# A two-layer graph network on one core: seven batches sum weighted input rows over the adjacency first and project the sums afterwards

## The chip, the core and the metric

The kernel runs on one core of a Trainium2 chip. Its engines each work through an instruction list of their own, in order: TensorE (PE, with its weight loads PEld) multiplies matrices into PSUM, VectorE (DVE), ScalarE (ACT) and GpSimd (POOL) work elementwise, SyncE (SP) issues nearly all transfers. Semaphores order the engines among each other. The metric is the device time of one execution in microseconds; lower is better.

## The reference, cut to what matters

Eight batches (B = 8) of N = 1024 rows with D = 128 features go through two layers, each followed by a residual and a layer norm.

```
# layer 0: masked attention
v, q, k = relu(x@Wv+bv), relu(x@Wq+bq), relu(x@Wk+bk)
att = softmax(q@k.T * adj - NEG*(1-adj))
x1 = layernorm(x + relu((att@v)@Wo + bo))
# layer 1: graph layer with additive logits
h = x1@W_w.T + W_b
e, f = h@a1, h@a2
u = adj * exp(e[:,None] + f[None,:] + a_b)
out = layernorm(x1 + (u / u.sum(axis=2)) @ h)
```

Since exp(e+f) is exp(e)·exp(f), layer 1 needs for each row n the sum over m of adj[n,m]·exp(f[m])·h[m] and the sum of the adj[n,m]·exp(f[m]) alone, its denominator.

## The kernel before

All orders are written out by hand, one list for each engine, in the functions `head` (batch 0, and what batch 1 needs of its projections), `batch_pass(p)` for p = 1 to 6, and `tail`. A pass works on the attention of batch p row block by row block (eight blocks of 128 rows), on the projections of batch p+1, and on what is left of the batches p-1 and p-2. LAST is 7.

**Attention.** `scores(p,i)` streams six 128x512 products (a high and a low part of q and k) into `s_ps`. DVE's `mask_max` adds the mask `penalty`, takes the maximum and writes `prob`; ACT's `probs` takes the exponential; `transpose_p(p,i,k)` turns four 128x128 blocks into `pt_ps[k]`; ACT's `prob_hi` and DVE's `prob_lo` split them; `attend(p,n)` runs 24 matmuls of 256 columns for two row blocks. `s_ps` and each `pt_ps[k]` exist once, so `scores(p,i+1)` waits for `mask_max(p,i)`, and `transpose_p(p,i+1,k)` for `prob_lo(p,i,k)`. ACT's `av_out` and PE's `project_out` follow, then on DVE `o_out`, `residual0` and the statistics of the first norm, POOL's `rstd0_pow`, DVE's `shift_mean0` and ACT's `norm0`, which leaves x1.

**Layer 1 of batch b.** `transpose_x1` turns x1 on PE (eight blocks), ACT's `x1t_out` takes it out, `project_h` multiplies with `w1` (128x130: the projection and the two columns of e and f), DVE's `h_out` copies, ACT's `exp_ef` takes the exponentials, `g_full` weighs each row of h with exp(f), and `g_hi`, POOL's `g_lo` and two small instructions for the denominator split that into the 258 columns of `g`. `aggregate(b,i)` (L1652) then holds a 128x128 block of the adjacency as the weights and streams the 258 columns, eight matmuls for each of the eight row blocks. DVE's `agg_out` (L1090) adds the two halves, `den_out`, `inv_den_out` and `scale_out` form the factor of each row, POOL's `residual1` (L450, L454) and `add_wb` (L445) apply it and add x1 and the bias, and statistics and `norm1` end the batch. ACT's `round_adj` makes each adjacency tile ready out of one of two staging buffers `adjt_in`; SP's `load_adj_t` fills one when it is free. The last batch does the same in pairs of row blocks, at the end of `tail`.

**Banks.** q, k, v, o, x1t, h and agg share three PSUM banks `m_ps` in the order of the `SLOTS` tables. **Queue.** SP issues in order; a load that waits for its buffer holds back all loads behind it.

## Time and profile before

| | us |
|---|---|
| median of 3 runs (395.12 to 395.23) | 395.15 |
| the profiled execution | 395.13 |
| its span, first to last instruction | 393.4 |
| PE busy | 380.5 (97%) |
| ACT busy | 329.9 (84%) |
| DVE busy | 292.8 (74%) |
| POOL busy | 279.9 (71%) |

The granted TensorE clock was 0.991 on average. Times inside the trace count from the start of the span; 1.7 us of the execution lie outside it. A matmul's own duration (290 ns for 256 columns) is longer than the distance to the next one, because matmuls overlap; what a stream costs is read from start to start.

### The profile page before, as it was taken

The page shows a single profiled execution, that of the slowest core. Times are in us where ns is not written, and L with a number is a line of the kernel's source. Part 1 is how long each engine was busy: PE and PEld are TensorE (multiplying, and loading weights), DVE is VectorE, ACT ScalarE, POOL GpSimd, SP SyncE. Part 2 cuts the span into 40 slices and gives each one's busy share as a digit, 9 for nine tenths or more (in the row PEclk, how much of TensorE's full clock was granted, in tenths as well). Part 3 has the DMA queues.
Part 4 walks back from the last instruction along what each step waited for, and adds up shares of the span by engine and source line. Part 5 has one row for each costly group of instructions (what it writes and reads, how often), then busy time and mean ns, then how long its engine had stood idle before and what let it go on. Part 6 is the DMA issues. An engine that isn't in the chain of part 4 may idle for free.

```text
span 393.4 us, 8653 instructions
## 1 busy us (share of the span) xinstructions
PE 380.5 (97%) x2757; PEld 355.2 (90%) x2757; DVE 292.8 (74%) x883; ACT 329.9 (84%) x661; POOL 279.9 (71%) x258
## 2 busy tenths in 40 slices
PE   8999999999999999999999999999999999999990
PEld 7798989989999999999999999999999999999990
DVE  3786796678668886777957887688867779697976
ACT  5877679987889887997879878898888969999962
POOL 1454951696458994789937998389956899576673
PEclk9999999999999999999999999999999999999996
DMA  8945533807657168754597266780676647978011
GB/s 259 376 166 166 164 129 137 328 38 268 200 185 314 61 235 260 262 203 171 175 292 298 84 240 215 243 322 13 253 214 233 252 162 285 386 224 282 4 55 53
DMA packets 38156, 80.71 MB, mean 205 GB/s; under 512 B 2785, under 2 KB 19681, under 8 KB 38113
## 3 DMA queue, kind: packets, MB, share of 16 engines
q1 hardware_dynamic: 37824, 80.03, 58.3%
q8 instruction: 23, 0.38, 0.4%
q10 hardware_dynamic: 288, 0.14, 0.1%
q14 instruction: 21, 0.16, 0.1%
HBM read 75.96 MB, written 4.19 MB: 204 GB/s over the span
## 4 chain that ended last, share of the span: by engine, by line
PE 91%; DVE 5%; issue 2%; POOL 0%; ACT 0%; POOLq 0%; DVEq 0%; ACTq 0%
PE pt_ps L1612 14%; PE m_ps L1660 13%; PE s_ps L1541 8%; PE av_ps L1625 8%; PE av_ps L1626 8%; PE av_ps L1624 8%; PE s_ps L1543 7%; PE s_ps L1542 7%; PE m_ps L1583 4%; PE m_ps L1649 3%; PE m_ps L1633 3%; PE m_ps L1541 2%; PE m_ps L1542 2%; PE m_ps L1543 2%; PE m_ps L1640 2%
## 5 line engine op out<-in xcount | busy, mean ns | idle before, releaser
L1033 DVE TENSOR_TENSOR prob_tl<-pt_ps,prob_th 128x512 fp32r<-128x512 f32 x128 | 85.5, 684 | 29.8 <-ACT prob_th L670 29.6
L1025 DVE CUSTOM_DVE_ANT_0 prob<-s_ps,penalty 128x1024 f32<-128x1024 f32 x64 | 78.0, 1218 | 30.8 <-PE s_ps L1543 26.2
L670 ACT ACTIVATE prob_th<-pt_ps 128x512 fp32r<-128x512 f32 x128 | 74.7, 596 | 21.0 <-PE pt_ps L1612 20.8
L405 POOL TENSOR_SCALAR penalty<-raw 128x1024 bf16<-128x1024 f32 x64 | 66.4, 1047 | 28.3 <-DMA raw<-in_adj_dram 13.2
L662 ACT ACTIVATE prob<-prob,neg_max 128x1024 f32<-128x1024 f32 x64 | 73.8, 1153 | 1.4 <-DVE neg_max L1025 1.3
L1624 PE MATMUL av_ps<-prob_th,vh 128*128 128x256 f32 x256 | 74.1, 290 | 0.0
L1612 PE MATMUL pt_ps<-rhs,prob 128*128 128x128 f32 x512 | 73.2, 273 | 0.0
L1626 PE MATMUL av_ps<-prob_th,vl 128*128 128x256 f32 x256 | 72.4, 283 | 0.0
L1625 PE MATMUL av_ps<-prob_tl,vh 128*128 128x256 f32 x256 | 72.4, 283 | 0.0
L607 ACT ACTIVATE adj_t<-adjt_in 128x1024 fp32r<-128x1024 f32 x56 | 59.3, 1061 | 11.2 <-PE m_ps L1660 11.1
L1612 PEld LDWEIGHTS pt_ps<-rhs,prob 128*128 128x128 f32 x512 | 60.1, 141 | 4.1
L1660 PE MATMUL m_ps<-g,adj_t 128*128 128x258 f32 x448 | 63.2, 288 | 0.0
L1660 PEld LDWEIGHTS m_ps<-g,adj_t 128*128 128x128 f32 x448 | 57.9, 190 | 1.5
L1541 PE MATMUL s_ps<-kh,qh 128*128 128x512 f32 x128 | 53.5, 418 | 0.7 <-DVE neg_max L1025 0.6
L1543 PE MATMUL s_ps<-kh,ql 128*128 128x512 f32 x128 | 50.3, 393 | 0.0
L1542 PE MATMUL s_ps<-kl,qh 128*128 128x512 f32 x128 | 50.1, 392 | 0.0
L1625 PEld LDWEIGHTS av_ps<-prob_tl,vh 128*128 128x128 f32 x256 | 49.0, 191 | 0.0
L1624 PEld LDWEIGHTS av_ps<-prob_th,vh 128*128 128x128 f32 x256 | 49.0, 191 | 0.0
L1626 PEld LDWEIGHTS av_ps<-prob_th,vl 128*128 128x128 f32 x256 | 48.9, 191 | 0.0
L450 POOL TENSOR_TENSOR gs<-gs,scale 128x512 f32<-128x512 f32 x14 | 14.6, 1040 | 35.4 <-DVE scale L1103 35.4
L1090 DVE TENSOR_REDUCE gs<-m_ps 128x129 f32<-128x258 f32 x59 | 24.4, 416 | 7.2 <-PE m_ps L1660 7.1
L1541 PEld LDWEIGHTS s_ps<-kh,qh 128*128 128x128 f32 x128 | 24.1, 188 | 5.7 <-DVE neg_max L1025 0.9
(139 smaller groups left out, 785.2 us busy)
## 6 DMA issues: line engine op xcount, KB each, us to landing
raw<-in_adj_dram SPq DMA_DIRECT2D x64, 512.0 KB, 5.6
adjt_in<-in_adj_t_dram SPq DMA_DIRECT2D x56, 512.0 KB, 3.9
x_in<-in_x_dram SPq DMA_DIRECT2D x8, 512.0 KB, 6.2
raw<-in_adj_t_dram SPq DMA_DIRECT2D x8, 512.0 KB, 5.7
out_dram<-out_sb SPq DMA_DIRECT2D x14, 256.0 KB, 4.5
xt_odd<-in_x_t_dram SPq DMA_DIRECT2D x8, 256.0 KB, 5.2
raw<-in_x_t_dram SPq DMA_DIRECT2D x7, 256.0 KB, 4.7
out_dram<-out_sb SPq DMA_DIRECT2D x4, 128.0 KB, 1.8
```

Source lines behind the costliest of these rows:

```text
L662: sc.activation(prob[i % 2][:, :], prob[i % 2][:, :], ACT.Exp, bias=neg_max[:, i:i + 1], scale=-1.0, accum_out=row_sum[b % 2][:, i:i + 1]) ...
L670: sc.activation(prob_th[n % 2][:, tiles(k), (i % 2) * P:(i % 2 + 1) * P], pt_ps[k][:, :].rearrange("p (c n) -> p c n", n=P), ACT.Copy).the ...
L1025: v.tensor_tensor_reduce(out=prob[i % 2][:, :], in0=s_ps[:, :, :].rearrange("p a n -> p (a n)"), in1=penalty[:, n % RING, :], scale=-1.0, ...
L1033: v.tensor_tensor(prob_tl[n % 2][at], pt_ps[k][:, :].rearrange("p (c n) -> p c n", n=P), prob_th[n % 2][at].bitcast(F32), ALU.subtract).th ...
L1541: pe.matmul(dst, lh, rh, start=True, stop=False)
L1542: pe.matmul(dst, lh, rl, start=False, stop=False)
L1543: return pe.matmul(dst, ll, rh, start=False, stop=True)
L1612: last = pe.transpose(blk(pt_ps[k], c), blk(prob[i % 2], k * TH + c), ident)
L1624: pe.matmul(av_ps[:, 0:PAIR], vh[:, c, :], th[:, c, :], start=(c == 0), stop=False)
L1625: pe.matmul(av_ps[:, 0:PAIR], vh[:, c, :], tl[:, c, :], start=False, stop=False)
L1626: last = pe.matmul(av_ps[:, 0:PAIR], vl[:, c, :], th[:, c, :], start=False, stop=(c == T - 1))
L1660: last = pe.matmul(a[:, 0:2 * G1], adj_tile(b, i)[:, c, :], g[:, c, :, :].rearrange("p a e -> p (a e)"), start=(c == 0), stop=(c == T - 1))
```

## The change

For the batches 0 to 6 the order of layer 1 is turned round. The adjacency sums the weighted rows exp(f)·x1 themselves; the sums, 128 features by 1024 rows, come out already transposed, and the projection is applied to them. `transpose_x1`, `x1t_out`, `project_h`, `h_out`, `g_hi_den`, `g_lo_den` and POOL's `residual1` and `add_wb` go for these batches.

- e and f are row products on DVE (`weigh`): sixteen multiply-and-add reductions a batch of a 128x128 tile of x1 with one of two constant tiles (`a_rows`), the result of each one column of `dots`.
- `g_full` writes 127 weighted feature columns and, in place of the last one, the weight exp(f) itself; the constant `w_sum` (128x129, from `raw_wd`) undoes this and carries the bias and the denominator. `form_sets` on PE, `place_rows` and `place_sets` on DVE make these constants once, in `head`.
- `aggregate` holds a 128x128 part of g (high or low) as the weights and streams 512 columns of the adjacency: four matmuls for each of eight tiles, two sums of 512 rows. The adjacency comes in another layout, in transfers of the same size. ACT's `sums_out` takes a sum out, `project_sum` multiplies it with `w_sum`.
- `den_out`, `inv_den_out` and `scale_out` now come for each pair of row blocks, 128x2, four of each a batch; `residual1` is a DVE instruction for each row block that reads PSUM. x1 has two buffers.
- All order lists and bank tables are written anew. The last batch keeps its method.

```diff
+            def weigh(b, k):
+                dve.wait_ge(x1_done, T * b + (k + 1) * TH)
...
+                for t in range(k * TH, (k + 1) * TH):
+                    for r in range(2):
+                        v.tensor_tensor_reduce(out=blk(x1t, 2 * (t % TH) + r), in0=x1_in[b % 2][:, t, :], in1=a_rows[r], scale=1.0,
+                                               scalar=0.0, op0=ALU.mult, op1=ALU.add,
+                                               accum_out=dots[:, t, r:r + 1]).then_inc(dots_done, 1)
...
+            def residual1(b, j):
...
+                for c in range(2):
+                    t = 2 * j + c
+                    last = v.scalar_tensor_tensor(out=gs[:, t, 0:D], in0=bank["p", b, j][:, c * G1:c * G1 + D],
+                                                  scalar=scale1[:, t:t + 1], in1=x1_in[b % 2][:, t, :],
+                                                  op0=ALU.mult, op1=ALU.add)
...
-                for c in range(T):
-                    last = pe.matmul(a[:, 0:2 * G1], adj_tile(b, i)[:, c, :],
-                                     g[:, c, :, :].rearrange("p a e -> p (a e)"), start=(c == 0), stop=(c == T - 1))
+                    for r in range(2):
+                        last = pe.matmul(a[:, :], g[:, 2 * c2 + c, r, 0:D], half(adj_tile(b, i), c),
+                                         start=(i % TH == 0 and c == 0 and r == 0), stop=(i % TH == TH - 1 and c == 1 and r == 1))
...
+            def project_sum(b, j):
+                pe.wait_ge(ut_done, 2 * b + j // 2 + 1)
+                out_rows = shared("p", b, j)
+                for c in range(2):
+                    last = pe.matmul(out_rows[:, c * G1:(c + 1) * G1], blk(ut, 2 * j + c), w_sum, start=True, stop=True)
...
+            def sums_out(b, h):
+                act.wait_ge(agg_full, T * b + TH * (h + 1))
+                sc.activation(half(ut, h), bank["agg", b, h][:, :], ACT.Copy).then_inc(ut_done, 1)
```

Of SP's list in a pass, two lines of it:

```diff
+                load_adj_t(p - 1, 0)
+                if there(p - 2):
+                    load_adj_t(p - 2, 7)
...
-                if there(p - 2):
-                    load_adj_t(p - 2, 7)
-                load_adj_t(p - 1, 0)
```

**PE in a pass**, from the projection of q of the next batch on (its rows read `m_ps<-xth,w_hl`), first before, then now; `s_ps` rows are `scores`, `pt_ps` rows `transpose_p`, and two full-precision rows are one `project_*` call.

```order
L1543 MATMUL m_ps<-xth,w_hl 128x512
L1660 MATMUL m_ps<-g,adj_t 128x258 x16
L1612 MATMUL pt_ps<-rhs,prob 128x128 x4
L1583 MATMUL m_ps<-wb,raw 128x128 x2
L1660 MATMUL m_ps<-g,adj_t 128x258 x8
L1612 MATMUL pt_ps<-rhs,prob 128x128 x4
L1541 MATMUL s_ps<-kh,qh 128x512
```

```order
L1567 MATMUL m_ps<-xth,w_hl 128x512
L1668 MATMUL m_ps<-adj_t,g 128x512 x8
L1565 MATMUL s_ps<-kh,qh 128x512
...
L1668 MATMUL m_ps<-adj_t,g 128x512 x4
L1636 MATMUL pt_ps<-rhs,prob 128x128 x4
L1678 MATMUL m_ps<-sets,ut 128x129 x2
```

Eight narrow matmuls a row block became four wide ones a tile, and the projection of the sums follows where there was none.

**DVE in a pass**, from `mask_max(p,5)` (the `ISA prob,neg_max` row) to behind `mask_max(p,6)`, first before, then now; `x1t,dots` rows are `weigh`, here four row blocks of it, each product followed by a read of the accumulator.

```order
L1025 ISA prob,neg_max<-s_ps,penalty 128x1024
L1025 ISA neg_max 128x1
L1033 TENSOR_TENSOR prob_tl<-pt_ps,prob_th 128x4x128
L1080 COPY h_sb<-m_ps 128x260
L1108 BN_STATS stat<-gs 128x6 x4
L1025 ISA prob,neg_max<-s_ps,penalty 128x1024
```

```order
L1004 ISA prob,neg_max<-s_ps,penalty 128x1024
L1004 ISA neg_max 128x1
L1012 TENSOR_TENSOR prob_tl<-pt_ps,prob_th 128x4x128
L1102 BN_STATS stat<-gs 128x6 x4
L1064 ISA x1t,dots<-x_in,sets 128x128
L1064 ISA dots 128x1
...
L1004 ISA prob,neg_max<-s_ps,penalty 128x1024
```

Between two `mask_max` one copy went and eight products with eight reads came; another eight stand between `mask_max(p,4)` and `mask_max(p,5)`.

**SP at the start**, first before, then now; `raw<-in_x_t_dram 128x256` are the two quarters of x that the first projections wait for, `raw<-in_adj_dram` is a 512 KB tile of the mask, `wb` holds weights.

```order
L275 DMA raw<-in_x_t_dram 128x256 x2
L281 DMA raw<-in_x_t_dram 128x512
L284 DMA wb<-in_pack_b_dram 128x640
L255 DMA raw<-in_adj_dram 128x1024 x2
L288 DMA x_in<-in_x_dram 128x8x128
L281 DMA xt_odd<-in_x_t_dram 128x512 x2
```

```order
L258 DMA raw<-in_adj_dram 128x1024
L278 DMA raw<-in_x_t_dram 128x256 x2
L284 DMA raw<-in_x_t_dram 128x512
L258 DMA raw<-in_adj_dram 128x1024
L287 DMA wb<-in_pack_b_dram 128x640
L258 DMA raw<-in_adj_dram 128x1024
```

A mask tile moved ahead of the quarters, and the weights moved behind a second tile, whose buffer has to be free first (POOL's first `convert` frees it).

## Rows read from the trace of the kernel before

**Rows 1.** Busy time by stretch (us; instructions in brackets), granted clock, DMA share.

```profile
131.50:177.83 46.33, 46.33 (x342) 43.58 (x341) 35.09 (x104) 39.98 (x80) 37.13 (x34) 1.00 0.62 217
...
345.00:366.00 21.00, 20.97 (x166) 20.20 (x166) 16.96 (x61) 20.97 (x37) 13.25 (x11) 1.00 0.71 231
366.00:380.00 14.00, 13.17 (x108) 12.40 (x106) 11.49 (x52) 12.55 (x41) 11.44 (x12) 1.00 0.01 2
```

**Rows 2.** PE in order of time: start, duration, line, tiles.

```profile
228.57 0.28 PE L1624 MATMUL av_ps<-prob_th,vh 128*128 128x256 f32 x1
...
231.45 0.40 PE L1541 MATMUL s_ps<-kh,qh 128*128 128x512 f32 x1
...
232.83 1.12 PE L1660 MATMUL m_ps<-g,adj_t 128*128 128x258 f32 x8
233.79 0.60 PE L1612 MATMUL pt_ps<-rhs,prob 128*128 128x128 f32 x4
234.22 0.61 PE L1633 MATMUL m_ps<-wb,av 128*128 128x128 f32 x4
234.67 0.60 PE L1612 MATMUL pt_ps<-rhs,prob 128*128 128x128 f32 x4
```

**Rows 3.** All engines at the start, in order of time (idle time before, releaser).

```profile
0.79 0.85 SPq L275 DMA_DIRECT2D raw<-in_x_t_dram  x2
...
3.51 0.95 ACT L616 ACTIVATE xth<-raw 128x256 fp32r<-128x256 f32 x2 [0.52 <-DMA raw<-in_x_t_dram]
...
4.76 0.55 PE L1541 MATMUL m_ps<-xth,w_hl 128*128 128x256 f32 x1
...
12.79 1.23 DVE L1025 CUSTOM_DVE_ANT_0 prob<-s_ps,penalty 128x1024 f32<-128x1024 f32 x1 [0.87 <-issue]
...
14.08 0.50 PE L1541 MATMUL s_ps<-kh,qh 128*128 128x512 f32 x1
...
15.91 1.23 DVE L1025 CUSTOM_DVE_ANT_0 prob<-s_ps,penalty 128x1024 f32<-128x1024 f32 x1 [0.88 <-PE s_ps L1543]
```

**Rows 4.** Busy time and, last, GB/s of the fourth microsecond.

```profile
3.00:4.00 1.00, 1.00 (x7) 1.00 (x6) 0.24 (x2) 0.42 (x1) 0.00 (x0) 1.00 1.07 372
```

**Rows 5.** DVE in order of time, in one pass.

```profile
226.31 1.12 DVE L1047 SCALAR_TENSOR_TENSOR m_ps<-m_ps,inv_sum,wb 128x128 f32<-128x128 f32 x4
227.34 1.21 DVE L1025 CUSTOM_DVE_ANT_0 prob<-s_ps,penalty 128x1024 f32<-128x1024 f32 x1
228.48 0.08 DVE L1025 DVE_READ_ACCUMULATOR2_ANT neg_max<- 128x1 f32 x1
228.48 0.42 DVE L1054 SCALAR_TENSOR_TENSOR x<-m_ps,x_in 128x256 f32<-128x256 f32 x1
228.93 0.87 DVE L1060 BATCH_NORM_STATS2 stat<-x 128x6 f32<-128x128 f32 x4
229.72 1.32 DVE L1033 TENSOR_TENSOR prob_tl<-pt_ps,prob_th 128x512 fp32r<-128x512 f32 x2
230.96 0.15 DVE L1039 RECIPROCAL inv_sum<-row_sum 128x2 f32<-128x2 f32 x1
231.03 0.40 DVE L1054 SCALAR_TENSOR_TENSOR x<-m_ps,x_in 128x256 f32<-128x256 f32 x1
```

**Rows 6.** DVE groups by line and shape: busy us, mean ns of one, idle before.

```profile
L1025 DVE CUSTOM_DVE_ANT_0 prob<-s_ps,penalty 128x1024 f32<-128x1024 f32 x64 | 78.0, 1218 | 30.8 <-PE s_ps L1543 26.2 <-PE pt_ps L1612 2.3 <-issue 2.0
...
L1090 DVE TENSOR_REDUCE gs<-m_ps 128x129 f32<-128x258 f32 x59 | 24.4, 416 | 7.2 <-PE m_ps L1660 7.1
...
L1047 DVE SCALAR_TENSOR_TENSOR m_ps<-m_ps,inv_sum,wb 128x128 f32<-128x128 f32 x64 | 18.8, 348 | 0.5 <-PE m_ps L1633 0.5
...
L1183 DVE SCALAR_TENSOR_TENSOR gs<-gs,scale,x1b 128x128 f32<-128x128 f32 x8 | 2.3, 346 | 0.0
```

**Rows 7.** The chain that ended last, in the tail: start, us, what.

```profile
365.79 0.60 DVE prob_tl L1033
...
374.85 0.41 PE m_ps L1669 x2
```

More of the change, by code:

```diff
@@ L811, in head @@
                 av_out(0, 1)
+                v_relu(1, 2)
+                k_out(1, 1)
                 prob_hi(0, 5, 0)
@@ L1325, in batch_pass @@
-                if there(p - 2):
-                    agg_out(p - 2, 4)
+                if there(p - 2):
+                    scale_out(p - 2, 0)
+                prob_lo(p, 2, 0)
+                inverse_sum(p, 0)
+                if there(p - 2):
+                    residual1(p - 2, 0)
+                v_bias(p + 1, 0)
+                mask_max(p, 4)
                 shift_mean0(p - 1)
                 if there(p - 2):
-                    agg_out(p - 2, 5)
-                inverse_sum(p, 0)
@@ L1340, in batch_pass @@
                 prob_lo(p, 3, 0)
                 if there(p - 2):
-                    inv_den_out(p - 2)
+                    residual1(p - 2, 1)
+                weigh(p - 1, 0)
+                inverse_sum(p, 1)
                 if there(p - 2):
-                    scale_out(p - 2)
+                    inv_den_out(p - 2, 2)
                 prob_lo(p, 3, 1)
+                if there(p - 2):
+                    scale_out(p - 2, 2)
+                if there(p - 2):
+                    residual1(p - 2, 2)
@@ L1408, in tail @@
+                residual1(LAST - 2, 0)
                 prob_lo(LAST, 2, 0)
[L1409 to L1411 removed]
+                prob_lo(LAST, 2, 1)
+                weigh(LAST - 1, 0)
                 mask_max(LAST, 4)
[L1413 to L1416 removed]
+                weigh(LAST - 1, 1)
                 prob_lo(LAST, 3, 0)
+                den_out(LAST - 2, 2)
@@ L1432, in tail @@
-                prob_lo(LAST, 5, 0)
+                mask_max(LAST, 7)
+                prob_lo(LAST, 5, 1)
+                inverse_sum_pair(2)
+                prob_lo(LAST, 6, 0)
+                stats0_pair(0)
                 mean_var1(LAST - 2, 1)
-                stats0_pair(0)
+                prob_lo(LAST, 6, 1)
+                o_out(LAST, 1)
+                residual0(LAST, 1)
                 var_eps1(LAST - 2)
-                prob_lo(LAST, 5, 1)
-                mask_max(LAST, 7)
@@ L1731, in form_w1, with form_sets @@
                 pe.matmul(av_ps[:, E1:2 * E1], wb_wide[:, :], rhs1[:, :], start=True, stop=True).then_inc(set_full, 1)
+            def form_sets():
+                pe.wait_ge(wd_ok, 4)
+                pe.wait_ge(wc_ok, 3)
+                out_rows = shared("set", 0, 1)
+                for r in range(2):
+                    pe.matmul(blk(out_rows, r), a_wide[:, r, :], raw_wc[:, :], start=True, stop=True).then_inc(set2_full, 1)
+                pe.matmul(blk(out_rows, 2), raw_wd[:, :], ident, start=True, stop=True).then_inc(set2_full, 1)
             def head():
```

1002 lines of the change are left out of this document (494 added, 508 removed), and 9 rows, old and new, of tables (HEAD_SLOTS, PASS_SLOTS).

## The prediction

> **What bounds the kernel now.** I read the busy time by stretch first [rows 1]. In one pass, 46.33 us long, PE is busy for all 46.33; ACT has 39.98, POOL 37.13, DVE 35.09, and the granted clock is 1.00. PE is thus the bound of the six passes, and what is taken from its list shortens them as long as no other engine becomes late. In the tail this changes: from 345 to 366 ACT is busy for 20.97 of 21.00 us, as full as PE, and from 365.8 to 374.8 the chain of waits begins with a DVE instruction and reaches PE only at 374.85 [rows 7]. A saving on PE there is worth nothing by itself. At the start the first projection of PE is at 4.76, behind ACT's copy of a quarter of x (3.51), which waited for its transfer [rows 3].
>
> **What PE loses and gets.** The costs go from start to start [rows 2]. Four transposes take 0.43 to 0.44, from 233.79 to 234.22; an aggregate of one row block (eight matmuls, 258 columns) takes 233.79 − 232.83 = 0.96; six products of 512 columns take 232.83 − 231.45 = 1.38, so 0.23 each; a full-precision call of two 128-wide blocks takes 234.67 − 234.22 = 0.45.
> - The transposes of x1: seven batches of two go, 14 × 0.44 = −6.2.
> - The sums: 56 × 0.96 = 53.9 becomes 224 matmuls × 0.229 = 51.3, so −2.6 to −2.8.
> - The projection: 28 calls of 0.45 become 28 calls of the same kind with 129 columns, 0.
> - The constants: three full-precision products in the head, half of 0.45 each, +0.7.
>
> The sum is **−8.3**. By place: pass 1 loses transposes and projections of batch 0, whose new projection comes later, −0.9 − 1.8 = −2.7; passes 2 to 6 lose 0.9 + 0.4 each, −6.4; the tail exchanges about the same; the head +0.7. A pass then has 45.0 of PE.
>
> **The head: +0.8.** A 512 KB mask tile now goes before the quarters of x. At 372 GB/s [rows 4] it takes 1.4 us, so the first projection can move from 4.76 to about 6.2. Also, the weights wait behind a second tile that needs a freed buffer. For this, ACT, DVE and PE get a new order in the head whose gain the trace doesn't show; PE is nowhere idle long after the first `mask_max` (12.79 to 15.91 is a loop of 1.83 for scores and start of `mask_max`, and 1.29 back [rows 3]). Bounds: 0, if the new order takes all of it back, and +2.5, if the 1.4 stay and the weights cost another microsecond. I take 0.8, nearer to a part regained.
>
> **The six passes: +1.2.** Other engines must keep up with a pass of 45.0.
> - ACT exchanges two copies of 128x512 (`x1t_out`) for two of the same size (`sums_out`): about 40 of 45, nothing to pay.
> - POOL loses two kinds of instruction and gets none: it is looser than before.
> - DVE loses eight `agg_out` of 0.416 [rows 6] and four copies of about the same width, −5.0. It gets eight `residual1` at 0.26 (four `o_out`, which read PSUM too, take 227.34 − 226.31 = 1.03), +2.1; some nine small instructions at 0.07 (230.96 to 231.03), +0.6; and sixteen `weigh`. All rows of this: [rows 5].
>
> What one `weigh` costs, call it w, no row shows: a multiply with a sum, 128 columns, both operands in SBUF, then a read of the accumulator. From below: a statistics instruction of 128 columns takes 0.79 / 4 = 0.20. `mask_max` (1024 columns, also with an accumulator read) takes 1.14 and `prob_lo` (512) 0.62, so 1.0 ns a column, and 1.14 − 896 × 0.00102 = 0.23 for 128 columns. In that place the read has a duration of 0.08, but the next instruction starts in the same instant, 228.48. From above: 0.26 as `o_out`, plus 0.08 if the read isn't overlapped, 0.34. I take 0.23, since `mask_max` is the nearest kind. So DVE has 35.1 − 5.0 + 2.1 + 0.6 + 16 × 0.23 = 36.5 of 45: on average loose.
>
> But the products stand in two lumps of eight, between `mask_max(p,4)` and `(p,5)` and between `(p,5)` and `(p,6)`, and scores and transposes have one buffer each. So I count one stretch: from the start of `scores(p,4)` to the end of the `prob_lo` that `transpose_p(p,5,1)` needs. DVE: 1.83 to the first `mask_max`, three of them 3.42, five `prob_lo` 3.1, eight small 0.56, a 256-wide step 0.42, four `residual1` 1.04, statistics 0.79, together 11.2 + 16 w. PE in the same stretch: three scores 4.14, five calls of 0.45, five groups of transposes 2.2, two `attend` of 231.45 − 228.57 = 2.88 [rows 2], one projection 0.69, together 15.0. With w = 0.23 DVE has 14.9: just in time. From w = 0.24 on each pass waits 16 (w − 0.24). As so little is left I add 0.2 us for small waits in each pass, 1.2 in all. Bounds: 0, and at w = 0.34, 6 × 1.6 = 9.6.
>
> A rule speaks against the new products here. Two instructions with the same 128 columns, one with an operand in PSUM (L1047) and one with both fp32 operands in SBUF (L1183), take 348 and 346 ns [rows 6]: the place of the operands changes nothing. The Trainium skill, "Vector Engine (DVE) Microarchitecture Reference", section 7 on points easy to get wrong, says that a two-input instruction of the scalar-tensor kind with two SBUF operands that are not bf16 runs at half throughput. These rows disagree with it.
>
> **The tail: +1.8.** ACT, full there, gets four `sums_out` (batches 5 and 6) for two `x1t_out`; two more of 512 columns at about 0.62 (DVE's 512-wide `prob_lo` [rows 5]), less a few small steps: +0.8 in 345 to 366. In the DVE stretch from 365.8 on, the `agg_out` of batch 6 leave, but eight `residual1` (2.1) and twelve small ones (0.8) come, behind a copy and a projection; I count a third of the 2.9, +1.0, on the chain. Bounds: 0 (all beside PE's last sums), and +2.9 + 0.8 = 3.7.
>
> **Forecast.** The profiled execution took 395.1 (span 393.4 and 1.7 around it), which is the median of the runs. 395.1 − 8.3 + 0.8 + 1.2 + 1.8 = **390.6**.
>
> **Rivals.**
> 1. *Everything is covered.* Head, waits and tail cost nothing: 395.1 − 8.3 = 386.8. For it: 8 us a pass spare on DVE and 5 on ACT. Against: ACT's full stretch in the tail, and the mask tile ahead of the quarters.
> 2. *Order and transfers eat the gain.* In five passes the load of the last adjacency tile of a batch now stands behind the first tile of the next. If `aggregate(p-2,7)` finds its tile late by up to a tile's 1.4 us, 0 to 7.0 is lost; from 0.9 a pass on hardly anything is left of the gain. Taken at 0.95: 390.6 + 4.7 = 395.3, no change. Against: PE reads a batch's eight tiles over a whole pass, so a tile is loaded long before its use; the DMA share in a pass is 0.62 [rows 1].
> 3. *The lump of `weigh` stops the score loop: slower.* The forecast's gain of 4.5 is used up at 96 (w − 0.24) = 4.5, w = 0.287. At w = 0.32 (`o_out` and most of the read) it is 390.6 + 7.7 = 398.3, and at 0.34 400.2. For it: the read of the accumulator comes here after each 128 columns, not after 1024, and nobody has seen it so close together. Against: 228.48, where it costs nothing.
> 4. *The products take two passes over their operands*, 128 × 1.0 ns = 0.13 more, w = 0.36: 390.6 + 96 × 0.12 = 402.1. Against: 346 and 348 ns. It is what the halving in that section of the Trainium skill would do here; no row bears it out.
>
> **Chances.** Forecast (388 to 393.5) 0.47; rival 1 0.20; rival 2 0.13; rival 3 0.17; rival 4 0.03. About 0.2% (0.8 us) is what a measurement of this kernel can tell from no change. Rival 2 lies on both sides of that band: about half in it, half still faster. So faster 0.73, same 0.07, slower 0.20. The range: below, rival 1 with a little more, 386.5; above, 398.5, which takes in w up to 0.32 and leaves out the rest of rivals 3 and 4, about 0.1 at either end.
>
> **What would show it.** In the profile after: a pass of 45.0 to 45.3 with PE busy in nearly all of it; sums at 0.23 a matmul; `weigh` at 0.23 from start to start. PE's first projection near 6 instead of 4.76. If w is 0.26 or more, PE waits in each pass for `neg_max` or for `prob_lo` around the blocks 5 and 6, and only there. If rival 2 holds, the last sum of a batch waits for ACT's `round_adj`, and that for a transfer. If the tail is mis-sized, the stretch from the last `prob_lo` of attention to the end, 393.4 − 365.8 = 27.6 now, has grown by something other than 1 us. I would be wrong most of all if the new order shortens a stretch that is not bound by PE, the head or the DVE stretch of the tail: I count no gain there.

## The result and the profile after

The changed kernel takes **407.72 us** (median of 4 runs, 404.39 to 409.53) against 395.19 of the kernel before: ratio 1.031, 95% interval 1.024 to 1.038. It is slower by 3.1%; I had said 390.6, in a range of 386.5 to 398.5. The profiled execution, the slowest of the four, took 409.53 (span 407.8; before 393.4). Its page, busy time, granted clock in 40 slices and the chain that ended last, by engine:

```profile
PE 381.2 (93%) x2483; PEld 336.9 (83%) x2483; DVE 320.8 (79%) x1141; ACT 332.0 (81%) x668; POOL 232.6 (57%) x223
...
PEclk9989999999999999999999999999999999999996
...
PE 47%; DVE 17%; DMA 11%; ACT 10%; issue 7%; POOL 1%; SPq 1%; DVEq 0%; POOLq 0%; ACTq 0%
```

The chain is the first thing to see. PE is still the fullest engine, but the chain runs through PE in 47% of the span only; before it was 91%. PE has gone from bound to one of several that wait for each other. The waits of PE, the largest and one more (line, what it waited for: us in total, times, longest):

```profile
PE m_ps L1668 <- ACT adj_t L589: 3.4, 3, 1.4
PE m_ps L1755 <- ACT raw L635: 3.2, 1, 3.2
PE m_ps L1565 <- DVE w_hl L1204: 2.4, 1, 2.4
...
PE m_ps L1678 <- ACT ut L669: 1.2, 2, 0.8
```

And by stretch, as [rows 1]: busy time, granted clock, DMA share.

```profile
0.00:10.00 10.00, 6.18 (x26) 5.37 (x27) 2.75 (x10) 4.23 (x7) 1.79 (x8) 0.92 0.69 229
10.00:20.00 10.00, 8.75 (x49) 7.04 (x47) 8.67 (x13) 6.67 (x13) 6.16 (x5) 0.90 0.76 272
20.00:30.00 10.00, 7.79 (x34) 6.44 (x35) 7.41 (x16) 5.33 (x11) 3.27 (x4) 0.83 0.52 174
...
256.70:303.70 47.00, 45.88 (x303) 40.69 (x302) 37.88 (x141) 40.27 (x80) 30.39 (x29) 1.00 0.59 208
```

In the first 30 us PE is idle for more than 7 and the granted clock is below 1.00; a pass of 47.00 has PE busy for 45.88.

A ruler for everything below: when PE starts the first `attend` of batch 0, 1 and 7, when it starts the last `attend`, and the span. Each is given against the kernel before (22.9, 61.5, 337.9, 367.3 and 393.4), from the profiled execution of each version. Batch 1 closes the head, batch 7 the six passes. It is one execution of each, and the same lists don't give the same times twice: with the head of the changed kernel left as it is, batch 0 stands at +10.3 (the changed kernel), +8.5, +9.8, +8.1 and +8.5 (`e4_swap`, `e5_port`, `e6_bench`, `e7_tail`). In this head a difference of under 2 us between single executions says little.

```
version      batch 0  batch 1  batch 7  last attend  span
after         +10.3     +8.4    +10.5      +9.9     +14.4
e1_loads       +6.7     +4.7     +7.1      +6.8     +11.0
e2_sets        +6.7     +5.4     +8.4      +7.9     +12.2
e3_head        +0.3     +3.5     +4.6      +3.8      +8.2
e4_swap        +8.5     +6.5     +5.4      +4.5      +8.5
e5_port        +9.8     +7.8     +5.0      +3.9      +7.9
e7_tail        +8.5     +6.5     +5.1      +5.1      +9.0
e8_head        +2.3     +2.1     +3.2      +2.3      +6.5
e9_stt         -0.4     +0.2     -0.9      -2.3      +1.8
e11_tail       +0.2     +0.8     -0.3      -1.7      +1.7
e12_all        +0.1     +0.6     -0.4      -0.2      +3.8
e14_act        +0.5     +1.0     -1.9      -2.3      +2.2
e13_order      -0.3     +0.3     -2.6      -3.2      +1.7
e15_all        +0.1     +0.7     -2.3      -2.7      +0.1
e16_all        -0.2     +0.3     -2.8      -2.7      -1.4
```

So of the 14.4 in this execution 8.4 come from the head, 2.1 from the six passes (where I expected −7.9), −0.7 from the last batch's attention, and 4.6 from what follows the last `attend`.

**The head**, all engines in order of time:

```profile
5.79 0.72 ACT L598 ACTIVATE xth<-raw 128x256 fp32r<-128x256 f32 x2 [2.80 <-DMA raw<-in_x_t_dram]
...
6.83 0.29 DVE L1204 TENSOR_TENSOR w_hl<-wa,w_hl 128x128 fp32r<-128x128 f32 x1
...
7.18 0.39 PE L1565 MATMUL m_ps<-xth,w_hl 128*128 128x256 f32 x1 [2.41 <-DVE w_hl L1204]
```

```profile
16.33 1.69 DVE L992 TENSOR_TENSOR ql<-raw,qh 128x512 fp32r<-128x512 f32 x1
17.95 2.29 DVE L1227 COPY a_wide<-wa 128x128 f32<-128x128 f32 x2
20.16 1.09 DVE L1228 TENSOR_SCALAR raw_wd<-wb 128x127 f32<-128x127 f32 x1
...
22.20 1.19 PE L1755 MATMUL m_ps<-raw_wc,a_wide 128*128 128x128 f32 x4 [3.23 <-ACT raw L635]
...
24.05 0.63 PE L1566 MATMUL s_ps<-kl,qh 128*128 128x512 f32 x1
24.47 0.63 PE L1567 MATMUL s_ps<-kh,ql 128*128 128x512 f32 x1
```

The first projection starts at 7.18 instead of 4.76 [rows 3], since ACT's quarter of x lands behind the mask tile and the split of the weights stands behind it on DVE. Then DVE makes the constants, slowly (two copies of 128 columns in 2.29; one at 7.92 took 0.22), and PE stands 3.23 us before `form_sets`. Behind that wait products of 512 columns come every 0.42 (24.05 to 24.47) where the same ones take 0.23 [rows 2]. The granted clock there (the third figure from the end) is 0.50, the lower of the two levels 1.2 and 2.4 GHz:

```profile
22.20:25.50 3.30, 3.29 (x11) 2.91 (x12) 2.10 (x5) 2.24 (x5) 1.05 (x1) 0.50 0.88 291
```

This doesn't follow every such wait. `e4_swap` has the same head and waits 2.26 at the same place, up to 21.88; behind it the clock is full:

```profile
21.90:26.00 4.10, 4.10 (x24) 3.29 (x25) 3.60 (x9) 2.81 (x6) 1.11 (x2) 1.00 1.00 356
```

**A pass**, SP, ACT and PE in order of time:

```profile
149.02 0.81 SPq L263 DMA_DIRECT2D adjt_in<-in_adj_t_dram  x2
```

```profile
154.87 1.06 ACT L589 ACTIVATE adj_t<-adjt_in 128x1024 fp32r<-128x1024 f32 x1 [1.64 <-DMA adjt_in<-in_adj_t_dram]
```

```profile
155.98 1.20 PE L1668 MATMUL m_ps<-adj_t,g 128*128 128x512 f32 x4 [1.05 <-ACT adj_t L589]
```

SP issues two adjacency tiles together, the first of the next batch ahead of the last of this one. ACT and then PE wait for the second one. The same stands at 250.12 (1.38) and 297.14 (0.93): this is my second rival, as I had described it.

### The profile page after: what moved, and what is told of

Read it like the earlier page. It is cut to its first block, busy times and chain, and to the rows that moved or that the text cites. A ratio compares the mean times of both kernels' runs of the same rounds, so it can differ in the third digit from the quotient of the medians.

```text
span 407.8 us, 8276 instructions
## 1 busy us (share of the span) xinstructions
PE 381.2 (93%) x2483; PEld 336.9 (83%) x2483; DVE 320.8 (79%) x1141; ACT 332.0 (81%) x668; POOL 232.6 (57%) x223
## 4 chain that ended last, share of the span: by engine, by line
PE 47%; DVE 17%; DMA 11%; ACT 10%; issue 7%; POOL 1%; SPq 1%; DVEq 0%; POOLq 0%; ACTq 0%
DMA adjt_in<-in_adj_t_dram 10%; PE pt_ps L1636 8%; PE m_ps L1668 6%; PE s_ps L1565 5%; PE s_ps L1566 4%; PE s_ps L1567 4%; ACT adj_t L589 4%; PE av_ps L1649 4%; PE av_ps L1648 4%; PE av_ps L1650 4%; DVE x1t L1064 3%; DVE prob L1004 3%; DVE prob_tl L1012 2%; PE m_ps L1657 2%; DMA raw<-in_adj_t_dram 2%
## 5 line engine op out<-in xcount | busy, mean ns | idle before, releaser
L1004 DVE CUSTOM_DVE_ANT_0 prob<-s_ps,penalty 128x1024 f32<-128x1024 f32 x64 | 78.1, 1220 | 35.9 <-PE s_ps L1567 29.9
L408 POOL TENSOR_SCALAR penalty<-raw 128x1024 bf16<-128x1024 f32 x64 | 67.4, 1059 | 36.5 <-DMA raw<-in_adj_dram 21.9
L1636 PE MATMUL pt_ps<-rhs,prob 128*128 128x128 f32 x512 | 75.0, 274 | 1.1 <-DVE prob_tl L1012 0.6
L1668 PE MATMUL m_ps<-adj_t,g 128*128 128x512 f32 x224 | 61.0, 408 | 3.4 <-ACT adj_t L589 3.4
L1565 PE MATMUL s_ps<-kh,qh 128*128 128x512 f32 x128 | 54.8, 428 | 1.3 <-DVE neg_max L1004 0.9
L427 POOL CAST kh<-raw 128x512 fp32r<-128x512 f32 x14 | 8.2, 615 | 78.1 <-PE s_ps L1567 78.1
L1668 PEld LDWEIGHTS m_ps<-adj_t,g 128*128 128x128 f32 x224 | 39.8, 189 | 12.6 <-ACT adj_t L589 5.2
L435 POOL TENSOR_TENSOR vl<-raw,vh 128x512 fp32r<-128x512 f32 x16 | 20.7, 1295 | 15.0 <-ACT vh L640 15.0
```

Source lines behind the costliest of these rows:

```text
L408: gp.tensor_scalar(penalty[:, n % RING, :], adj_in[:, n % RING, :], PENALTY, -PENALTY, ALU.mult, ALU.add).then_inc(penalty_done, 1)
L1004: v.tensor_tensor_reduce(out=prob[i % 2][:, :], in0=s_ps[:, :, :].rearrange("p a n -> p (a n)"), in1=penalty[:, n % RING, :], scale=-1.0, ...
L1565: pe.matmul(dst, lh, rh, start=True, stop=False)
L1636: last = pe.transpose(blk(pt_ps[k], c), blk(prob[i % 2], k * TH + c), ident)
L1668: last = pe.matmul(a[:, :], g[:, 2 * c2 + c, r, 0:D], half(adj_tile(b, i), c), start=(i % TH == 0 and c == 0 and r == 0), stop=(i % TH == ...
```

## The experiments

Beside each the kernel before ran on the same chip (395.0 to 395.2).

**The head: three undos.** `e1_loads` gives SP's list at the start its old order:

```diff
 def head():   # SP
-    load_adj(0, 0)
-    load_x_t_quarter(1)
     load_x_t_quarter(0)
+    load_x_t_quarter(1)
     load_x_t(0, 1)
...
```

> The changed kernel, with only SP's load order of the head put back to the order of before (quarters of x first, weights early). Theory (the head lost 10.3 us, by three separate causes: late quarters and weights, constants in DVE's way, and the half clock that follows each wait of PE): the first projection moves from 7.18 back to about 5, the slow stretch of matmuls from 8.6 to 11.6 goes, the wait of 3.2 us for form_sets stays; the first attend moves from 33.2 to 29.5 or 30, time about 404. Rival (the loads are covered by the later waits of the head): the first projection moves, the first attend stays within 1 us of 33.2, time 407 to 408.

405.79, ratio 1.027 (1.024 to 1.030). `e2_sets` only moves `place_rows`, `form_sets` and `place_sets` to the end of the head:

> The changed kernel, with the making of the constants (place_rows and place_sets on DVE, form_sets on PE) moved from the start of the head to its end. Theory (DVE's three copies of the constants, slowed beside POOL to about 1 us each, hold back v_bias, the second mask_max and so PE for 3.2 us, and the half clock that follows costs another 1.5): first attend from 33.2 to about 28.5, time about 403. Rival (it is the slow stretch of DVE beside POOL, whatever stands there): less than 2 us of it come back, 406 or more.

405.08, 1.024 (1.021 to 1.026). In these executions batch 1 comes 3.7 and 3.0 earlier; in the medians the kernels gain 1.9 and 2.6, and their intervals overlap with that of the changed kernel. Both times missed the theory (404 and 403) and lie between it and the rival. `e1_loads` still waits 2.85 before `form_sets`, but with the full clock behind it, so a part of its gain may be the clock's. Neither run alone settles a cause; what follows does. `e3_head` has the whole head of before, with the constants late:

> The changed kernel with the whole head in the order of before on all five engines, the constants behind it (place_rows late in the head, form_sets at its end, place_sets in pass 1). Theory (the head's order alone is worth 9 to 10 us): the first attend is at 23 to 24, and the gain is kept: time 398 to 399, still over 395, since passes gain nothing and the tail loses. Rival (the lists of pass 1 need the new head, or the passes take it back by waits of their own): over 402.

403.70, 1.022 (1.020 to 1.023): batch 0 as forecast (+0.3), batch 1 at +3.5, so the time missed the expected 398 to 399 by 5 us and is the rival's. The constants had found the next bad place, in front of a `mask_max` that PE waits for. DVE:

```profile
35.58 1.33 DVE L1227 COPY a_wide<-wa 128x128 f32<-128x128 f32 x1
36.83 1.09 DVE L1228 TENSOR_SCALAR raw_wd<-wb 128x127 f32<-128x127 f32 x1
```

Here too each of them takes over 1 us. `e8_head` (with the swap of `e4_swap`, below) lets ACT make the constants:

```diff
 def head():   # ACT
     q_out(0, 1)
+    place_rows()      # as activations
 def head():   # PE
     transpose_p(0, 0, 1)
+    form_sets()
```

> The load order of e4_swap, the whole head in the order of before, and the constants made on ACT (five small instructions behind the second q_out), the three products behind the first transposes. Theory (the head loses by order, and by DVE making constants beside POOL): no wait of PE over 0.5 us in the head, the first attend at 23.5 to 24, that of batch 1 at 62.5 to 63 where e3_head had 65.0; time 398.5. Rival (the lists from pass 1 on need the other head): batch 1 at 64 or later, 400 or more.

399.12, 1.010 (1.008 to 1.012), near the 398.5 of the theory and 6.4 us better than `e4_swap`. A wait of 1.56 was left right behind `form_sets`; with that put to the end of the head (in `e9_stt`) batch 1 is at +0.2. The 8.4 us of the head were the order, and which engine makes the constants; the half clock went with them.

**The passes: two loads.** `e4_swap`, two lines of SP's list:

```diff
+    if there(p - 2):
+        load_adj_t(p - 2, 7)
     load_adj_t(p - 1, 0)
-    if there(p - 2):
-        load_adj_t(p - 2, 7)
```

> The changed kernel with two lines of SP's list of a pass in the order of before: the load of the last adjacency tile of a batch ahead of the first one of the next batch. Theory (the load of tile 7 waits behind one that needs a later round_adj, and shares the queue with it: 1.05, 1.38 and 0.93 us of waiting on PE in three passes): these three waits go, time 404 to 405. Rival (another wait ends a little later in the same place, PE's list is held by DVE or ACT): the waits for adj_t go, the period of the passes stays, 407.

405.48, 1.027 (1.022 to 1.033). The medians are 2.2 apart and the intervals overlap; in the profiled executions, all passes at a granted clock of 1.00, the six passes go from +2.1 to −1.1 in the table. The three waits are gone, but a pass is 46.65 (three from 167.82 to 307.76), longer than before. What is left are two waits in each pass, 0.38 for `prob_tl` and 0.36 for `neg_max`. Just ahead of them, DVE and POOL:

```profile
209.18 0.28 DVE L1064 CUSTOM_DVE_ANT_0 x1t<-x_in,sets 128x128 f32<-128x128 f32 x1
...
209.38 1.12 DVE L1064 CUSTOM_DVE_ANT_0 x1t<-x_in,sets 128x128 f32<-128x128 f32 x1
...
210.43 0.28 DVE L1064 CUSTOM_DVE_ANT_0 x1t<-x_in,sets 128x128 f32<-128x128 f32 x1
```

```profile
209.20 1.15 POOL L464 TENSOR_TENSOR out_sb<-out_sb,rstd 128x512 f32<-128x512 f32 x1
```

Fifteen products start 0.21 apart, one takes 1.05, and it ends when POOL's normalisation ends. `e5_port` moves that POOL instruction from there:

```diff
     norm1(p - 3, 0)
+    norm1(p - 3, 1)
     v_lo(p, 1)
...
     q_lo(p + 1, 0)
-    norm1(p - 3, 1)
     k_hi(p + 1, 0)
```

> The load order of e4_swap, and on POOL the second half of norm1 of a pass moved directly behind its first half, away from the time in which DVE runs the first eight products of weigh. In e4_swap one product of each pass took 1.12 us in place of 0.28 and ended with POOL's norm1 instruction, and PE then waited for prob_lo and neg_max, 1.17 us a pass beyond its work. Theory (a DVE instruction with both operands in SBUF waits for POOL's running instruction, and that makes the stall): no product of weigh near 209 is long, the two waits shrink from 1.17 to under 0.4 a pass, about 4 us less than e4_swap, time 400 to 401. Rival (DVE is simply too full there, w is over 0.24): the long product goes, and the waits of PE stay over 0.8 a pass, 404 or more.

403.59, 1.024 (1.018 to 1.031, widened by one run of 408.96); a pass 46.20 instead of 46.65, the long product gone, one wait of 0.2 a pass left. The mechanism is as the theory has it; the 400 to 401 was missed: the six passes gained 1.6 (−1.1 to −2.8 in the table), not 4.

**What POOL holds on DVE.** `e6_bench` puts rows of DVE instructions behind the kernel's end, alone and beside POOL (482.3 with them).

> The changed kernel with extra DVE and POOL work on scratch tiles behind its end: seven forms of DVE instruction (weigh, a copy, statistics, scalar-tensor with one PSUM operand, the same with two SBUF operands, a 512-wide subtraction with one PSUM operand and one with two SBUF operands), first alone, then beside a row of 24 POOL subtractions of 512 columns, then beside 24 POOL converts. Its total says nothing on the change. Theory (DVE and POOL exclude each other where DVE reads two SBUF operands or copies in SBUF, not where one operand is in PSUM): weigh 0.21 alone and about 1.2 beside POOL, the copy and the two-operand forms likewise, the forms with a PSUM operand and the statistics as fast as alone. Rival (a general contention): all forms get slower by a like factor, none waits for a whole POOL instruction.

DVE alone, then beside POOL's 512-wide subtractions, then (last row) beside its `convert`; what one instruction of a row costs is read from start to start:

```profile
403.69 0.28 DVE L1264 CUSTOM_DVE_ANT_0 x1t<-x_in,sets 128x128 f32<-128x128 f32 x1
...
403.90 1.17 DVE L1267 COPY ut<-x_in 128x128 f32<-128x128 f32 x8
...
416.95 1.33 DVE L1264 CUSTOM_DVE_ANT_0 x1t<-x_in,sets 128x128 f32<-128x128 f32 x1 [1.37 <-POOL xtl L490]
...
418.22 1.34 DVE L1264 CUSTOM_DVE_ANT_0 x1t<-x_in,sets 128x128 f32<-128x128 f32 x1
...
427.09 9.81 DVE L1267 COPY ut<-x_in 128x128 f32<-128x128 f32 x8
436.82 1.63 DVE L1269 BATCH_NORM_STATS2 stat<-x_in 128x6 f32<-128x128 f32 x8
438.37 2.14 DVE L1271 SCALAR_TENSOR_TENSOR gf<-m_ps,minus_half,x_in 128x128 f32<-128x128 f32 x8
440.43 2.18 DVE L1274 SCALAR_TENSOR_TENSOR xt_odd<-x_in,minus_half 128x128 f32<-128x128 f32 x8
...
470.76 4.74 DVE L1274 SCALAR_TENSOR_TENSOR xt_odd<-x_in,minus_half 128x128 f32<-128x128 f32 x8
```

A copy of 128 columns goes from 0.14 to 1.22, a product of `weigh` from 0.21 to 1.27: each stands for a whole POOL instruction (1.24). Statistics (0.20) and the form that reads PSUM (0.26) don't change. The Trainium skill, "SBUF — State Buffer", section "SBUF: two separate sides", says that the two engines share a pair of ports under a lock that lasts a whole instruction, taken by VectorE in a two-port mode or with two SBUF inputs, and that whichever starts first has it. The copy and the product agree with it. So does the last form (two SBUF inputs), with the roles changed: beside the subtractions it keeps its 0.27, and it is POOL that waits, two subtractions in 4.51 instead of 2.48:

```profile
438.00 2.48 POOL L490 TENSOR_TENSOR ql<-prob 128x512 fp32r<-128x512 f32 x2
440.45 4.51 POOL L490 TENSOR_TENSOR kl<-prob 128x512 fp32r<-128x512 f32 x2
```

Beside `convert` it takes 0.59. Why the copy loses in such a row and this form wins, no run shows; and it doesn't always win, as `e15_all` shows below. The kernel before had the effect too, in its tail. A shift of two columns, also a scalar-tensor instruction with two SBUF operands, took 0.93 beside POOL, where the next one takes 0.13 (375.55):

```profile
368.66 1.19 POOL L454 TENSOR_TENSOR gs<-gs,x1b 128x512 f32<-128x512 f32 x1
368.94 0.93 DVE L1143 SCALAR_TENSOR_TENSOR shift<-mv,rstd 128x2 f32<-128x2 f32 x1
```

Is it the product's special instruction? `e9_stt` (`e8_head`, `form_sets` late, and the products as the ordinary form):

```diff
-v.tensor_tensor_reduce(out=..., in0=x1_in[...], in1=a_rows[r], scale=1.0, scalar=0.0,
-                       op0=ALU.mult, op1=ALU.add, accum_out=dots[:, t, r:r + 1])
+v.scalar_tensor_tensor(out=..., in0=x1_in[...], scalar=1.0, in1=a_rows[r],
+                       op0=ALU.mult, op1=ALU.mult, accum_out=dots[:, t, r:r + 1])
```

> As e8_head (load order of e4_swap, head of before, constants made on ACT; here the three products that form the constants stand late in the head, before the second q projection of batch 1), and weigh written as a scalar-tensor-tensor instruction with a sum in place of the custom multiply-and-reduce. The bench showed the custom form to wait for a whole POOL instruction each time (1.27 us in place of 0.21) and the scalar-tensor form with the same two SBUF operands not to (0.26 beside POOL subtractions). Theory (the stall of the passes is this exclusion, not the number of products): with 0.26 a product, dearer than 0.21 alone, the long product of 1.1 us goes, and so do most of the waits of 1.17 us a pass for prob_lo and neg_max; the passes go from 46.65 to 46.0 or less, time 396 to 397. Rival (DVE is too full, a product of 0.26 makes it worse): the waits stay or grow, the passes stay at 46.6 or more, 399 or more.

398.04, 1.007 (1.005 to 1.010). The product still starts 0.21 after the other, and one in a pass still takes 1.12 (156.61, 203.22, 249.86, 296.47); PE's waits are what they were. My theory on the form fell: with a constant as scalar and a sum as second result the ordinary form waits for POOL too. What the profile shows as gained is 1.9 in the head, and a wait of 1.40 at 331.14 in `e8_head`, for an adjacency tile that landed late.

**The tail.** After the last `attend` come 30.6 us instead of 26.0. `e7_tail` (on `e4_swap`) gives the last batch its own `ef` tile and puts the products of its first two pairs into the two score banks, the first pair ahead of the last `attend`:

```diff
-            ("h_last", LAST, 0), ("x1t", LAST, 2), ("h_last", LAST, 1), ("o", LAST, 3), ...
+            ("x1t", LAST, 2), ("o", LAST, 3), ...
+        bank["h_last", LAST, 0], bank["h_last", LAST, 1] = s_ps[:, 0, :], s_ps[:, 1, :]
```

> The load order of e4_swap, and in the tail the exponentials of the last batch in a tile of their own (so that they need not wait for the factors of the batch before), and the products of its first two pairs in the two score banks, the first ahead of the last attend (so that they need not wait for residual1 of the batch before). Theory (the tail's 3.9 us are the last batch's chain held up by the sums of batch 6 through one tile and three shared banks): the stretch from the last attend to the end goes from 30.0 in e4_swap to 27 or 28, time 403. Rival (DVE's added work of batch 6 is the bound there, whatever the banks): under 0.8 us, 405.

405.69, 1.026 (1.023 to 1.029); 29.9 us remain, as the rival has it. But a new wait of 2.15 for `residual0` stands at 382.62 in this execution, with the clock at 0.50 behind it, so the run alone doesn't show that tile and banks cost nothing. `e11_tail` (`e9_stt` with the first form of `weigh`) takes POOL's normalisation of batch 6, beside which DVE's short instructions took about 1 us, to ACT:

```diff
-    norm1(LAST - 1, 0)      # POOL
-    norm1(LAST - 1, 1)
+    norm1_rows(0)           # ACT, behind g_hi_pair(3)
...
+    norm1_rows(1)
```

> As e9_stt but with the custom weigh again, and norm1 of batch 6 moved from POOL to ACT (eight scalings with a bias, as the last batch has them), so that POOL runs no 512-wide instruction beside DVE's small ones at the end. Theory (the tail lost 3.9 us mostly because POOL's norm1 of batch 6, which came later with the projection of the sums, now runs beside the last chain and holds DVE's small SBUF instructions, five of 0.7 to 1.0 us in place of 0.15): those five are short, the stretch from the last attend to the end goes from 30.0 to 27 or 27.5, time 396. Rival (DVE's own added work is the bound): they are short, but the stretch stays over 29, 398 or more.

396.82, 1.005 (1.004 to 1.007); 29.5 us remain, again as the rival has it, though the time is nearer to the theory's. `e12_all` joins all of this:

> All parts that helped together, on the method of the change: the load order of e4_swap, the head of before with the constants made on ACT, POOL's norm1 away from weigh as in e5_port, and a tail in which norm1 of batch 6 is on ACT, the last batch's exponentials have their own tile and the score banks, and DVE does the last residual0 ahead of the statistics of batch 6. Theory (the method saves some 8 us of PE's work, and what ate it are order, exclusion of DVE and POOL, and waits): passes at 46.1 or less, the stretch from the last attend to the end 27.5 or less, time 391.5 to 393, under before. Rival (DVE's added work is the bound of the passes and of the tail, so the method is worth nothing here): 395 or more.

397.71, 1.006 (1.004 to 1.008). Missed by 5: batch 6's attention starts 1.4 earlier than in `e11_tail`, and the tail lost it in four waits of 0.83 to 1.31. Its trace named them: ACT's copies `round_adj` and `round_last` stood waiting for their transfers in front of steps that PE needed, and DVE had batch 6's statistics in front of the last batch's `g`. `e14_act` moves only those ACT copies (three places like this one):

```diff
-    round_adj(LAST - 2, 6)
     sums_out(LAST - 2, 0)
     probs(LAST, 1)
+    round_adj(LAST - 2, 6)
```

> The version with all repairs (shown above: 397.71, profiled 398.92, span 397.2), with ScalarE's list alone changed at three places of the tail: a copy that rounds an adjacency tile and stood waiting for its transfer (1.83 us at 325.66, 1.07 at 334.81, 0.69 at 364.08) goes behind the steps that others wait for (sums_out, probs, prob_hi). Theory (late engines in front of TensorE, not TensorE's own work, make the tail longer): TensorE's waits of 1.21 at 327.3, 0.41 at 337.2 and 0.83 at 366.3 go; the start of the last attend moves from 367.1 to about 365; from there to the end 30.1 as now, since VectorE's list is untouched: 395.5 to 396.5. Rival (the last batch's own chain sets the end, and what ends before it counts for nothing): the last attend moves, the end does not: 397.5.

397.19, 1.005 (1.004 to 1.007). The last `attend` came 2.1 earlier than in `e12_all`, the span shrank by 1.6, the median by 0.5: between the theory (395.5 to 396.5) and the rival (397.5), nearer to the rival. `e13_order` also takes batch 6's statistics off that stretch of DVE and gives the last batch its own result tiles:

```diff
-    stats1(LAST - 1, 0)      # DVE, behind residual1(LAST - 1, 1)
...
     var_eps0_pair(3)
+    stats1(LAST - 1, 0)
     g_lo_den_pair(2)
     g_lo_pair(2)
+    stats1(LAST - 1, 1)
```

> As the run with ScalarE's list changed, and also: VectorE's statistics of batch 6 (16 bn_stats and bn_aggr and what follows, 2.4 us) move out of the stretch between the last attention and the last batch's g into the gaps behind it (2.4 us of them from 377 to 381), for which the last batch gets its own result tiles. Theory (in that stretch VectorE is the bound, because batch 6's residual and denominators came into it: 2.1 + 0.6 us more than before): TensorE's waits of 1.31 at 377.1 and 1.29 at 382.3 go, from the last attend to the end 27.5 to 28 instead of 30.1, 26.1 before the change; time 392.5 to 394, below the 395.0 of the kernel before. Rival (TensorE's and ScalarE's own work there sets the length): 29.5 or more from the last attend to the end, 395 to 396.

396.91, 1.005 (1.004 to 1.007). Both DVE waits went and the last batch's first sum came at 373.45 (375.48 in `e14_act`, 377.14 in `e12_all`), but the end stayed, because a third wait took their place. PE, then a stretch with its clock:

```profile
375.52 0.71 PE L1714 MATMUL m_ps<-w,x1t 128*128 128x130 f32 x4 [1.34 <-ACT x1t L707]
375.99 0.91 PE L1746 MATMUL s_ps<-g,adjt_last 128*128 128x258 f32 x4
376.69 1.06 PE L1746 MATMUL pt_ps<-g,adjt_last 128*128 128x258 f32 x4
377.55 1.06 PE L1746 MATMUL s_ps<-g,adjt_last 128*128 128x258 f32 x4
```

```profile
375.50:379.00 3.50, 3.48 (x19) 3.48 (x20) 2.68 (x14) 3.47 (x14) 0.86 (x1) 0.62 0.01 2
```

Behind a wait of 1.34 four products take 0.86 instead of 0.48, at a granted clock of 0.62. `e15_all` takes this wait away (ACT's `norm0_pair(1)` and `round_last(6)` later), gives the last results a tile of their own and puts POOL's power for batch 6 ahead of its additions:

```diff
     x1t_out_pair(2)
-    norm0_pair(1)
     exp_ef_pair(2)
...
     g_hi_pair(3)
+    norm0_pair(1)
```

> As the run with VectorE's statistics moved (396.9, span 395.1: VectorE's waits in front of TensorE were gone there and the first product of the last batch came at 373.45 instead of 377.14, but a copy of x1 on ScalarE, held 1.71 us by norm0_pair(1), kept TensorE waiting 1.34 at 375.52, behind which the products ran at 0.215 instead of 0.12 until 379; at 389.86 ScalarE waited 3.27 for a store of batch 6). Three repairs: norm0_pair(1) and the copy of adjacency tile 6 go behind the steps that TensorE waits for; POOL makes batch 6's deviation ahead of its additions; the last batch's results go to a tile of their own. Theory (late engines, one behind the other, and the half clock that follows a wait, are all that separates this version from the saving): TensorE's waits of 0.87 at 369.3 and 1.34 at 375.5 go, with the slow stretch 3.5 us in all, of which part is lost to the chain at the end: 392.0 to 393.5, first version below the kernel before (395.0). Rival (the last chain on VectorE from the first sum to the end, 14.4 us in e13_order and 12.8 before, stays bound to its own instructions): 395 to 396.

395.28, 1.000 (0.999 to 1.001): even with the kernel before, not below it, as the rival has it. In the last chain two DVE instructions stood beside POOL's additions:

```profile
380.35 1.25 DVE L1217 SCALAR_TENSOR_TENSOR shift<-mv,rstd 128x8 f32<-128x8 f32 x1 [0.16 <-POOL rstd L464]
...
381.79 1.45 DVE L1197 SCALAR_TENSOR_TENSOR gs_l<-gs_l,scale,x_in 128x128 f32<-128x128 f32 x2
```

```profile
380.28 2.54 POOL L454 TENSOR_TENSOR x_in<-x_in,wb_row 128x512 f32<-128x512 f32 x2
```

Without POOL beside them the shift takes 0.16 (`e13_order`, 383.15) and two such residuals 0.59 (383.96). The residual is the form that kept its 0.27 in `e6_bench`, with a scalar from a tile and two SBUF operands.

`e16_all`:

```diff
-    rstd1_pow(LAST - 1)      # POOL
     add_wb(0)
+    rstd1_pow(LAST - 1)
...
-    round_last(6)            # ACT
     exp_ef_pair(3)
...
-    shift6()                 # DVE, ahead of scale_pair(0)
     stats1_pair(0)
+    shift6()
```

> As e15_all (395.3; no wait of TensorE but 1.00 at 377.85 is left in the tail, and TensorE ends its work at 382.6, 1.1 earlier than before the change, but the end is the same). In VectorE's last chain two instructions stood beside POOL's addition of 380.2 to 381.5: the shift of batch 6 took 1.25 instead of 0.16 and a residual 1.45 instead of 0.60. Changed: the copy of adjacency tile 6 behind the last exponentials (TensorE's wait of 1.00), the shift of batch 6 behind the first statistics of the last chain, POOL's first addition ahead of its power. Theory (VectorE held by POOL, and one late copy, are what is left): 1.0 + 1.1 + 0.9 less what comes new: 392.5 to 393.5, below the kernel before (395.0). Rival (the end is set by the length of the last chain itself, about 12.5 us from its first sum): the first sum can come at most 1.0 earlier: 394.3.

**393.72** (393.46 to 393.94), ratio 0.9966 (0.9954 to 0.9978): between theory and rival, nearer to the theory, and the first version that beats both kernels, the one before by 0.3%. Its page and the largest waits of PE behind the preparation of 1.4 us, which the kernel before has too:

```profile
PE 376.6 (96%) x2483; PEld 334.6 (85%) x2483; DVE 316.5 (81%) x1138; ACT 334.8 (85%) x681; POOL 227.0 (58%) x219
...
PE 66%; DVE 20%; issue 6%; ACT 3%; DMA 2%; SPq 1%; POOL 1%; DVEq 0%; POOLq 0%; ACTq 0%
```

```profile
PE s_ps L1581 <- DVE neg_max L1027: 1.1, 4, 0.4
PE s_ps L1581 <- DVE ql L1015: 0.9, 1, 0.9
PE s_ps L1744 <- DVE g L1171: 0.4, 1, 0.4
```

Even here the chain runs through PE in 66% only. And the 1.4 us are not the method's alone: several of the repairs (batch 6's norm on ACT, the last batch's own tiles, the later copies) don't depend on it, and no run gives them to the kernel before.

## Why the prediction was wrong

By place, in the profiled execution: the passes +2.1 where I had −7.9, the head +8.4 where I had +1.5 (0.8 and the constants' 0.7), the tail +3.9 where I had +1.8. So the six passes are the step that failed most (by 10.0), then the head (6.9), then the tail (2.1). In all three I priced the waits too low, and in the passes the saving too high.

**PE's saving, −8.3: too large.** `e16_all` hardly waits, so its steady pass (46.16, from 199.66 to 245.82) can be set against one of before (46.32, 200.94 to 247.26), start to start, idle time taken out:

```
in one pass                  before        e16_all
transposes of x1              0.87            -
sums                          8.04           7.68
projection (16 products)      1.63           1.87
everything else              35.78          36.39
idle                          0.00           0.22
```

Transposes and sums are as I counted them (−0.87 and −0.36 against −0.87 and −0.4; 56 × 0.96 is 53.8, not 53.9, which is little). The projection, which I set at 0, costs +0.24; so the pass has −1.0 of work where I wrote −1.3. Then the same products of attention and projections take 0.60 more from start to start, 0.41 of it in the scores and 0.19 in `attend`, and 0.22 is idle: −0.16 a pass is left. Over all six passes `e16_all` is 3.1 shorter than before, 1.2 of it in the first and 1.2 in the last.

**The passes, +1.2 of waits: 2.1 lost where −7.9 was forecast.** Of the 10.0 the two lines of SP's list are 3.3 (`e4_swap`) and POOL's instruction beside `weigh` 1.6 (`e5_port`); the other 5.1 are mostly saving that even `e16_all` doesn't show (−3.1 against −7.9). Two causes of waits, one of them on my list.
- Rival 2 (0.13) was right in mechanism and place: three waits of 0.93 to 1.38. My reason against it, that "a tile is loaded long before its use", is refuted by 154.87: the tile was used as soon as it landed. ACT frees a staging buffer at 148.99, and only then, at 149.02, SP can issue.
- Rival 3's place was right and its mechanism wrong. w is 0.21 from start to start (I took 0.23), the read of the accumulator costs nothing, and no second pass over the operands shows, so rivals 3 and 4 fall as written (`e6_bench`: eight scalar-tensor instructions with one operand in PSUM 2.14, with both in SBUF 2.18). But one product of sixteen stood 1.05 beside POOL. That is 0.84 in a stretch that I had at 14.9 against 15.0, "just in time"; in `e4_swap` PE's waits there came to 0.74 a pass. The trace of before had a sign of it that I overlooked (0.93 at 368.94, beside POOL), and I counted POOL only as "looser than before".

**The head, +0.8: 8.4.** I saw the mask tile ahead of the quarters and priced it at 1.4 of transfer; the first projection came 2.4 later. I named 0 and +2.5 as bounds from the transfer alone and let "the new order" of the other engines take some back. The order was the cost: the wait of 3.23 before `form_sets`, DVE's constants beside POOL, and, in this execution, half clock behind the two long waits. `e8_head` and `e9_stt` show it by undoing it (+2.1 and +0.2).

**The tail, +1.8: 3.9 (−0.7 and +4.6).** The added work on DVE was counted too low: `residual1` costs what I had (four take 1.02, from 380.20 to 381.22), but the twelve small instructions take 2.0 from start to start where I had 0.8; one of them stood 0.62 beside POOL. The share on the chain (a third) was too low too. `e14_act` and `e13_order` bear it out in part: the late copies cost the last batch's first sum 1.7, the statistics ahead of it 2.0. But the end followed only in part: the spans shrank by 1.6 and 0.5. Neither shared tiles, nor POOL, nor DVE alone was enough; each time another engine was late next, and only all of it together (`e16_all`) shortened the tail to 27.3, still 1.3 over before.

**What I had right:** the bound before, the price of a sum, w, and the place of the lost time in a pass (PE waiting around the blocks 5 and 6). That the idea in itself saves time isn't shown beyond the 3.1 us of the passes in `e16_all`.

Open is why the changed kernel varies so much from run to run (404.39 to 409.53, `e16_all` 0.5). A part is the clock: of the five executions with the same head, two have half clock behind the wait before `form_sets`, and their batch 0 is the latest (+10.3 and +9.8, against +8.1 to +8.5). Why it fell there and not in the others no run shows. Open also is why scores and `attend` start 0.60 a pass later.

## What to carry to other kernels

When the bound engine is 100% busy, taking work off it can make the other engines' orders the bound, as here: price the new slack of each against each wait, not against the average, and expect to get a part of it. Before counting small VectorE instructions at their own duration, look at what GpSimd runs at that moment; a 0.2 us instruction can take 1.2. And a long wait of the matrix engine can cost more than its length: in some executions, not in all, its clock is at half behind it.

## What the runs showed of the hardware

- In rows of eight, VectorE's copy and its product with a sum, both from SBUF, wait for a whole GpSimd instruction each (0.14 and 0.21 become 1.22 and 1.27; `e6_bench`), and single small instructions from SBUF in the kernels do too (0.13 becomes 0.93 in the kernel before, 0.16 becomes 1.25 in `e15_all`); statistics and forms that read PSUM don't (0.20, 0.26 with and without).
- Rows of VectorE instructions with two SBUF operands and no sum aren't slowed beside GpSimd's subtractions (0.27, and 0.62 at 512 columns); there GpSimd waits, two subtractions in 4.51 and 4.82 instead of 2.48. Single ones are slowed: two residuals of 128 columns took 1.45 instead of 0.59 beside its additions (`e15_all`).
- After waits of 3.23, 2.41, 2.15 (`e7_tail`) and 1.34 us (`e13_order`) products ran at half clock (0.42 instead of 0.23; 0.215 instead of 0.12). After waits of 2.26 (`e4_swap`), 2.85 (`e1_loads`) and 1.38 (a pass) the granted clock stayed at 1.00: the length of the wait doesn't decide it alone.
